# Scattering token numbers instead of token rows for a mixture of experts, and placing the skew rows in nine groups

## The chip, the cores and the metric

The kernel runs on one core of one Trainium2 chip. The metric is the device time of one execution in microseconds (us), the median of several runs; one further execution was taken with the hardware profiler, and every number of the trace comes from that one.

## The reference

Three transformer layers and a last rotation work on x of shape (4, 512, 288), so 2048 tokens of 288 numbers in float32. Each layer has attention with 16 heads and a feed-forward part of width 1152, both modulated by a condition. Only layer 0 matters to the change, where the feed-forward part is a mixture of 4 experts, and each token goes to its best 2:

```python
xn = _modulate(_ln(x), sh_mlp, sc_mlp)
xf = xn.reshape(-1, C)
gate_logits = xf @ w_gate
topk_logits, topk_idx = jax.lax.top_k(gate_logits, TOP_K)      # TOP_K = 2
gates = jax.nn.softmax(topk_logits, axis=-1)
cw = jnp.sum(one_hot(topk_idx, NUM_EXPERTS) * gates[..., None], axis=1)
hmid = gelu(jnp.einsum('tc,ech->eth', xf, w1) + b1[:, None, :])
eo = jnp.einsum('eth,ehc->etc', hmid, w2) + b2[:, None, :]
moe = jnp.einsum('te,etc->tc', cw, eo).reshape(B, N, C)
return x + g_mlp[:, None, :] * moe
```

The last rotation needs two more things that are prepared during the layers. U is the orthogonal factor of a QR factorization of P (288 x 64), which GpSimd makes with 64 Householder reflectors. R is expm(A), where A (one 64 x 64 skew-symmetric matrix for each batch) has its 2016 entries above the diagonal from a small product with L3_cond_W.

## The kernel before

Five engines run their own programs, written out in order by hand, and meet at semaphores; nothing reorders them. SP (SyncE) issues nearly all DMAs, GpSimd (POOL in the profile) issues the indirect ones.

**Layer 0, attention.** Work goes in 16 groups (4 batches, 4 groups of heads). SP loads each group's stacks of q and k (load_stacks, L732 and L733) and puts the row maxima into them (place_max, L772); TensorE makes scores for the maximum (L1448) and for the softmax (L1462); ScalarE takes the exponential (L1223); TensorE multiplies with v (L1473). Layers 1 and 2 run the same code. In layer 0 alone ScalarE also issues clear_rows (L1210) once in each group: 16 DMAs that write zeros from UO, still empty then, over all 9728 rows of the buffer XSD ("moe_rows_d").

**Layer 0, routing.** For each batch in turn the normalized rows XMR are made, VectorE counts the slot of each token with each of its two experts (slots, L2185, which gives IDX), and GpSimd scatters the 1152-byte rows into XSD with 8 indirect DMAs of 128 rows (scatter, L944). The rows of an expert then lie together, and spare slots hold zeros. tile_table makes the first row and the expert of 11 tiles of 512 slots.

**Layer 0, experts.** The 11 tiles (TILES) have 9 units each (HM), 99 units j in all. SP loads a tile's rows with one DMA (load_rows, L622) into one of two buffers XROW, and its weights in thirds, each as soon as VectorE has split the third before (load_tile_w1, load_tile_w2). Iteration t of SP's loop loads for tile t + 2. VectorE's program, unit by unit: the low part of the hidden numbers (L2262); in unit 1 tile_tails of the next tile (L2245, the first reader of its rows) and tile_take of the tile before (L2271); in units 2 to 4 the rows' split (L2253); in units 2, 5 and 8 the low parts of the next tile's w1 thirds (L2375, L2376). It also makes the skew entries from unit 4 (SKEW_UNIT, L2424; the first waits for l3_W and what is loaded behind it), the expm steps from unit 64 (EXPM_UNIT; step 0 on TensorE is L1727), and adds the experts' outputs back: combine(k, b) (L2280) for the first two batches at units 49, 57, 82 and 88 (COMBINE_UNIT). SP stores each tile's output (store_tile, L645), and GpSimd gathers the outputs by token for the combines (gather, L954). READY says how many tiles must be stored for it.

GpSimd fills the rest of its time with the reflectors, each of some 20 small instructions that depend on one another and one DMA (L867). PIVOTS cuts the 64 reflectors into pieces between its other work: 0 to 11 before the scatters, 12 to 18 before gather(0,0), 19 before gather(1,0), 20 to 26 before gather(0,1), and so on.

The skew entries are stored to DRAM in iteration 4 and come back with 63 DMAs, one per row of the triangle, to UO (place_skew, L651): 21 at the end of each of SP's iterations 4, 5 and 6.

Of the kernel before, what the change touches and what calls it, by code (L numbers as in the profile page):

```python
# [54 lines left out]
SKEW_UNIT, EXPM_UNIT = 4, 64  # L55
FRONT_SKEW = 4
FRONT = 12 + 2 * FRONT_SKEW
PIVOTS = (0, 12, 19, 20, 27, 28, 64)
# [14 lines left out]
def build(nc, x, cond, layers, l3_P, l3_W, l3_b, out):  # L73
    ctx = ExitStack()
    with ctx:
# [72 lines left out]

        STRICT = at("strictly_behind", [P, P], F32, rb + 58368)
# [76 lines left out]
        IDX = new("row_slots", [P, NT, 2], U32)  # L226
        TBL = new("tile_table", [P, 24], I32)
# [28 lines left out]
        XSD = nc.dram_tensor("moe_rows_d", [MOE_ROWS, C], F32, kind="Internal").ap()  # L256
# [83 lines left out]
        s_sd = sem("rows_scattered")  # L340
        s_zr = sem("rows_cleared")
# [197 lines left out]
        def _(sp):  # L539
# [103 lines left out]
            def store_tile(t):  # L643
                sp.wait_ge(m_ev, TT * (t + 1))
                sp.dma_start(YD[N * t:N * t + N, :].rearrange("(t p) c -> p t c", p=P), T1[:, :, :]).then_inc(m_y, 16)  # L645
# [6 lines left out]

            def moe_loads():

                sp.wait_ge(s_tb, 1)
                e = tile_expert(1)
                sp.wait_ge(s_sd, 32 * 16)
                load_rows(0)
                load_tile_w1(1, 0, e)
                load_rows(1)  # L660
                load_tile_b2(1, e)
                for i in range(3):
                    if i >= 1:
                        load_tile_w1(1, i, e)
                    load_tile_w2(1, i, e)
# [5 lines left out]
                for t in range(TILES):  # L671
# [20 lines left out]
                    if t == 4:  # L692
                        sp.wait_ge(s_vc, 1)
                        sp.dma_start(VD.rearrange("b (p t) -> p b t", t=VT_), VC[:, :, :]).then_inc(s_vd, 16)
                        sp.wait_ge(s_vd, 16)
                        sp.wait_ge(s_zr, 16 * B * HG)
                    if 4 <= t <= 6:
                        place_skew(range(21 * (t - 4), 21 * (t - 3)))
# [137 lines left out]
        def _(gp):  # L836
# [80 lines left out]
            def route_constants():  # L917
# [4 lines left out]
                gp.wait_ge(s_cn, 2)  # L922
                gp.affine_select(out=STRICT[:, :], in_=STRICT[:, :], compare_op=ALU.is_gt, fill=0.0, base=0,
# [13 lines left out]
            def scatter(b):  # L937
                if b == 0:
                    gp.wait_ge(s_zr, 16 * B * HG)
                gp.wait_ge(s_xc, 3 * b + 3)  # L940
                gp.wait_ge(s_ix, b + 1)
                for t in range(TT):
                    for k in range(2):
                        gp.indirect_dma_start(out=XSD[:, :], out_offset=bass.IndirectOffsetOnAxis(ap=IDX[:, TT * b + t, k:k + 1], axis=0),  # L944
                                              in_=XMR[b][:, t, :], in_offset=None).then_inc(s_sd, 16)
# [37 lines left out]
            reflectors(PIVOTS[5], PIVOTS[6])  # L983
# [1688 lines left out]
```

## Time and profile before

| | us |
|---|---|
| median of 3 runs | 1828.39 |
| lowest, highest | 1827.14, 1837.69 |
| the profiled execution's own time | 1825.07 |
| its span | 1823.3 |
| PE busy in the span | 1567.6 (86%) |
| DVE busy | 1304.7 (72%) |
| ACT busy | 936.6 (51%) |
| POOL busy | 732.0 (40%) |

PE is TensorE, PEld its weight loads, DVE VectorE, ACT ScalarE. An engine's name with a q (SPq, ACTq) is its queue, where DMAs are issued. The busy time tells how full an engine is over the whole span; the stages have different limits, so the rows below look at stretches. Times in a timeline count from the start of the span.

### The profile page before, as it was taken

The numbers are of one execution on the slowest core, as the hardware profiler recorded it, in microseconds if no ns is written. First come the engines' busy times: TensorE is split into PE (matmuls) and PEld (weight loads), VectorE is DVE, ScalarE is ACT, GpSimd is POOL, SyncE is SP. The second block draws the span as 40 slices with busy tenths as digits, with TensorE's granted clock in tenths as the row PEclk, the third lists the DMA queues.
The fourth block names the chain that finished last, engine by engine and source line by source line (L and its number), as shares of the span: only waits on it lengthen the run. The fifth ranks groups of instructions, "written<-read, shape, count | busy, mean of one in ns | idle before, by whom it ended". The sixth has DMA issues, their size and how long they took to land.

```text
span 1823.3 us, 29022 instructions
## 1 busy us (share of the span) xinstructions
PE 1567.6 (86%) x9053; PEld 1005.1 (55%) x9053; DVE 1304.7 (72%) x2364; ACT 936.6 (51%) x1657; POOL 732.0 (40%) x1607
## 2 busy tenths in 40 slices
PE   6878787766499996999967999989899899988998
PEld 4622222355488885788743222368787322248885
DVE  7776566544679767566687888777897888867763
ACT  4636566524355654344643777742255577772222
POOL 0566510024566346750366666566676600000000
PEclk9989889987699999999978999999999899999999
DMA  6566645601665544442435333421105422400001
GB/s 171 129 168 109 109 103 105 116 27 53 167 178 129 163 145 100 98 111 81 138 83 152 75 78 78 94 41 5 18 4 167 109 79 78 127 1 1 1 1 52
DMA packets 133684, 166.06 MB, mean 91 GB/s; under 512 B 34354, under 2 KB 115236, under 8 KB 133433
## 3 DMA queue, kind: packets, MB, share of 16 engines
q1 hardware_dynamic: 111802, 139.71, 26.6%
q0 software_dynamic: 5120, 13.65, 7.1%
q10 hardware_dynamic: 16640, 11.21, 3.5%
q8 instruction: 61, 1.00, 0.2%
q14 instruction: 61, 0.50, 0.1%
HBM read 113.97 MB, written 46.13 MB: 88 GB/s over the span
## 4 chain that ended last, share of the span: by engine, by line
PE 52%; DVE 20%; DMA 8%; SPq 8%; issue 7%; ACT 3%; POOL 1%; another core or an unknown queue 0%; DVEq 0%; ACTq 0%; POOLq 0%
PE psum L1324 15%; PE psum L1473 7%; PE psum L1462 7%; PE psum L1448 6%; PE psum L1625 6%; PE psum L1711 4%; DMA k_stack<-qk_parts_d 3%; DVE minus_max L2029 2%; SPq L732 2%; SPq L733 2%; SPq L772 2%; DMA q_stack<-minus_max_t 1%; DVE bn L1937 1%; PE psum L1518 1%; DVE x_norm L1959 1%
## 5 line engine op out<-in xcount | busy, mean ns | idle before, releaser
L2029 DVE TENSOR_REDUCE minus_max<-psum 128x2 bf16<-128x1024 f32 x384 | 453.5, 1219 | 137.8 <-PE psum L1448 130.9
L1223 ACT ACTIVATE probs<-psum 128x512 f32<-128x512 f32 x768 | 419.7, 601 | 211.8 <-PE psum L1462 209.6
L1462 PE MATMUL psum<-q_stack,k_stack 109*128 109x512 bf16 x768 | 266.9, 395 | 15.6 <-DMA q_stack<-minus_max_t 8.6
L1448 PE MATMUL psum<-k_stack,q_stack 108*128 108x512 bf16 x720 | 228.2, 400 | 49.6 <-DMA k_stack<-qk_parts_d 39.8
L1324 PE MATMUL psum<-x_split,w_hi 128*128 128x512 f32 x684 | 254.5, 413 | 10.8 <-DVE x_tail L1976 3.7
L874 POOL TENSOR_TENSOR qr_m<-qr_m 64x8 f32<-64x8 f32 (+35 forms) x544 | 204.5, 376 | 42.6
L1462 PEld LDWEIGHTS psum<-q_stack,k_stack 109*128 109x128 bf16 x768 | 73.9, 99 | 260.9 <-ACT probs L1223 179.5
L1473 PE MATMUL psum<-probs,v_stage 128*32 128x512 f32 x1536 | 208.3, 616 | 1.1 <-ACT o_t L1204 1.1
L1324 PEld LDWEIGHTS psum<-x_split,w_hi 128*128 128x128 f32 x684 | 130.7, 191 | 39.0 <-issue 9.5
L869 POOL TENSOR_TENSOR qr_m<-qr_rows 64x288 f32<-64x288 f32 (+31 forms) x64 | 45.8, 716 | 248.5 <-DMA qr_rows<-qr_rows 248.5
L1448 PEld LDWEIGHTS psum<-k_stack,q_stack 108*128 108x128 bf16 x720 | 69.0, 100 | 131.7 <-issue 40.2
L1324 PE MATMUL psum<-x_split,w_lo 128*128 128x512 f32 x342 | 136.3, 398 | 0.0
L1134 ACT ACTIVATE hid_f<-psum 128x512 f32<-128x512 f32 x99 | 59.2, 598 | 141.4 <-PE psum L1324 128.5
L1279 ACT ACTIVATE hid_f<-psum 128x512 f32<-128x512 f32 x72 | 42.9, 596 | 168.9 <-PE psum L1324 164.0
L1625 PE MATMUL psum<-w_hi,hid_hi 128*128 128x288 f32 x396 | 118.7, 300 | 11.8 <-DVE branch L2271 8.4
L2262 DVE TENSOR_TENSOR hid_lo<-hid_f,hid_hi 128x512 fp32r<-128x512 f32 x99 | 74.7, 755 | 66.6 <-ACT hid_hi L1099 61.4
L1625 PE MATMUL psum<-w_hi,hid_lo 128*128 128x288 f32 x396 | 117.7, 297 | 0.0
L1625 PE MATMUL psum<-w_lo,hid_hi 128*128 128x288 f32 x396 | 117.7, 297 | 0.0
L1324 PE MATMUL psum<-x_split,wqkv_hi 128*128 128x512 f32 (+1 forms) x240 | 94.7, 436 | 25.5 <-DVE qk_r L2014 22.1
L1711 PE MATMUL psum<-w_hi,hid_hi 128*128 128x288 f32 x288 | 87.1, 303 | 3.8 <-DVE hid_lo L2391 3.3
L1625 PEld LDWEIGHTS psum<-w_hi,hid_hi 128*128 128x128 f32 x396 | 75.3, 190 | 19.8 <-issue 10.9
L1711 PE MATMUL psum<-w_lo,hid_hi 128*128 128x288 f32 x288 | 85.2, 296 | 0.0
(354 smaller groups left out, 3242.1 us busy)
## 6 DMA issues: line engine op xcount, KB each, us to landing
qk_parts_d<-qk_parts SPq DMA_DIRECT2D x36, 384.0 KB
raw_b<-in_L_cond_w SPq DMA_DIRECT2D x30, 432.0 KB, 3.4
raw_a<-in_L_cond_w SPq DMA_DIRECT2D x30, 384.0 KB
moe_rows_d<-skew_upper ACTq DMA_DIRECT2D x16, 684.0 KB, 9.9
q_stack<-qk_parts_d SPq DMA_DIRECT2D x48, 216.0 KB
k_stack<-qk_parts_d SPq DMA_DIRECT2D x48, 216.0 KB
q_stack<-qk_parts_d SPq DMA_DIRECT2D x48, 144.0 KB
k_stack<-qk_parts_d SPq DMA_DIRECT2D x48, 144.0 KB
```

Source lines behind the costliest of these rows:

```text
L869: step(gp.tensor_tensor(QM1[:, 0, 0:n], rows, pivot, ALU.mult))
L874: step(gp.tensor_tensor(QM1[:, :, 0:h], QM1[:, :, 0:h], QM1[:, :, n - h:n], ALU.add))
L1134: act.activation(HF[:, j % 2, :], bk(j % 2), ACT.Gelu_apprx_tanh).then_inc(m_g, 1)
L1223: act.activation(PE_[:, v // 4, v % 4, :], psum[:, score_bank(v), :], ACT.Exp, scale=SCALE).then_inc(s_e, 1)
L1324: i = pe.matmul(dst, a, r, start=(n == 0), stop=(n == len(terms) - 1))
L1448: mm = pe.matmul(psum[:, 2 * (u % 2) + j, :], Q6[0:STK, g, u // 2, P * qt:P * qt + P], K6[0:STK, g, u // 2, :], start=True, stop=True)
L1462: pe.matmul(psum[:, score_bank(v), :], K6[0:STK + 1, g % 4, h, P * kt:P * kt + P], Q6[0:STK + 1, g % 4, h, :], start=True, stop=True).then ...
L1473: mm = pe.matmul(psum[32 * h:32 * h + 32, 6, :], VST[:, g % 4, kt, h, :], PE_[:, kt, h, :], start=(kt == 0), stop=(kt == TT - 1))
L1625: mm = pe.matmul(psum[:, 4 + q, 0:C], h[:, m % 3, c], w[:, m, :], start=(m == 0 and n == 0), stop=(m == HM - 1 and n == 2))
L1711: mm = pe.matmul(psum[:, 4 + t, 0:C], h[:, m % 3, c], w[:, m, :], start=(m == 0 and n == 0), stop=(m == HM - 1 and n == 2))
L2029: dve.tensor_reduce(MX[:, g % 2, 2 * u:2 * u + 2], psum[:, o:o + 2, :], AX.X, ALU.max, negate=True).then_inc(s_mx, 1)
L2262: dve.tensor_tensor(HL[:, m % 3, :], HF[:, j % 2, :], HH[:, m % 3, :].bitcast(F32), ALU.subtract).then_inc(m_h, 1)
```

## The change

- XSD is gone. The normalized rows are stored in token order with four plain DMAs (XTD), and the scatter writes 4-byte token numbers (TID, from an iota) into a small table SLD of 9728 slots. One DMA of SP clears SLD at the start; clear_rows is gone.
- SP loads a tile's 512 token numbers (load_tokens in place of load_rows), four to a partition, and GpSimd gathers the rows from XTD with four indirect DMAs per tile (gather_rows). Slots lie otherwise in the tile, and store_tile stores accordingly.
- GpSimd's order in the expert stage: gather_rows(t) for each tile, with one or two reflectors after each (PIVOTS new), gather(0,0) after the rows of tile 7 and gather(1,0) after those of tile 8.
- place_skew comes in nine groups of seven rows, between weight loads of iterations 4 to 6; its wait for the clear is gone. EXPM_UNIT goes from 64 to 66.

```diff
-SKEW_UNIT, EXPM_UNIT = 4, 64
+SKEW_UNIT, EXPM_UNIT = 4, 66
-PIVOTS = (0, 12, 19, 20, 27, 28, 64)
+PIVOTS = (0, 12, 13, 15, 17, 19, 20, 21, 22, 23, 24, 25, 64)
...
-            def load_rows(t):
+            def load_tokens(t):
                 if t >= 2:
-                    sp.wait_ge(m_tr, 3 * (t - 1))
-                sp.dma_start(XROW[t % 2][:, :, 0:C], XSD[tile_rows(t), :].rearrange("(t p) c -> p t c", p=P)).then_inc(m_x[t % 2], 16)
+                    sp.wait_ge(m_x[t % 2], 16 * TT * (t // 2))
+                sp.dma_start(TIX[t % 2][:, :], SLD[tile_rows(t), :].rearrange("(p t) o -> p (t o)", t=TT).bitcast(U32)).then_inc(m_ix[t % 2], 16)
...
+            def skew_rows(t, i):
+                if (t, i) == (4, 0):
+                    sp.wait_ge(s_vc, 1)
+                    sp.dma_start(VD.rearrange("b (p t) -> p b t", t=VT_), VC[:, :, :]).then_inc(s_vd, 16)
+                    sp.wait_ge(s_vd, 16)
+                if 4 <= t <= 6:
+                    first = 21 * (t - 4) + 7 * i
+                    place_skew(range(first, first + 7))
+
             def moe_loads():
+                for b in range(B):
+                    sp.wait_ge(s_xc, 3 * b + 3)
+                    sp.dma_start(XTD[N * b:N * b + N, :].rearrange("(t p) c -> p t c", p=P), XMR[b][:, :, :]).then_inc(s_xd, 16)
                 sp.wait_ge(s_tb, 1)
                 e = tile_expert(1)
                 sp.wait_ge(s_sd, 32 * 16)
-                load_rows(0)
-                load_tile_w1(1, 0, e)
-                load_rows(1)
+                load_tokens(0)
+                load_tokens(1)
...
                         load_tile_w1(t + 2, 0, e)
-                        load_rows(t + 2)
+                        load_tokens(t + 2)
                         load_tile_w2(t + 2, 0, e)
+                        skew_rows(t, 0)
                         load_tile_w1(t + 2, 1, e)
+                        skew_rows(t, 1)
                         load_tile_w2(t + 2, 1, e)
+                        skew_rows(t, 2)
                         load_tile_w1(t + 2, 2, e)
...
+            sp.wait_ge(s_cst, 2)
+            sp.dma_start(SLD.rearrange("(p n) o -> p (n o)", p=D3), UO[:, :, :].rearrange("p b d -> p (b d)")[:, 0:MOE_ROWS // D3].bitcast(I32)).then_inc(s_zr, 16)
...
+            def gather_rows(t):
+                if t == 0:
+                    gp.wait_ge(s_xd, 16 * B)
+                if t >= 2:
+                    gp.wait_ge(m_tr, 3 * (t - 1))
+                gp.wait_ge(m_ix[t % 2], 16 * (t // 2 + 1))
+                for q in range(TT):
+                    gp.indirect_dma_start(out=XROW[t % 2][:, q, 0:C], out_offset=None, in_=XTD[:, :],
+                                          in_offset=bass.IndirectOffsetOnAxis(ap=TIX[t % 2][:, q:q + 1], axis=0)).then_inc(m_x[t % 2], 16)
...
-            reflectors(PIVOTS[1], PIVOTS[2])
-            gp.wait_ge(s_iy, 1)
-            gather(0, 0)
-            reflectors(PIVOTS[2], PIVOTS[3])
-            gather(1, 0)
-            reflectors(PIVOTS[3], PIVOTS[4])
+            gather_rows(0)
+            gather_rows(1)
+            for t in range(2, TILES):
+                gather_rows(t)
+                if t == 7:
+                    gp.wait_ge(s_iy, 1)
+                    gather(0, 0)
+                if t == 8:
+                    gather(1, 0)
+                reflectors(PIVOTS[t - 1], PIVOTS[t])
             gather(0, 1)
-            reflectors(PIVOTS[4], PIVOTS[5])
+            reflectors(PIVOTS[TILES - 1], PIVOTS[TILES])
             gather(1, 1)
...
-            def clear_rows(bb, g):
...
-                    if v == 4 and l == 0:
-                        clear_rows(B - 1 if first else bb, HG - 1 if first else g - 1)
```

## Rows read from the trace of the kernel before

**Rows 1.** Busy time by stretch: attention 0, attention 1; clock, DMA share, GB/s.

```profile
116.30:365.90 249.60, 201.42 (x1031) 61.10 (x1029) 153.71 (x179) 146.53 (x271) 73.11 (x196) 0.88 0.60 111
993.50:1185.20 191.70, 186.25 (x1031) 59.04 (x1031) 156.56 (x182) 145.00 (x271) 115.24 (x312) 0.98 0.36 79
```

**Rows 2.** Groups by line, same stretches: busy, mean ns, idle before.

```profile
L1448 PE MATMUL psum<-k_stack,q_stack 108*128 108x512 bf16 x224 | 74.6, 417 | 38.2 <-DMA k_stack<-qk_parts_d 38.1
...
L1448 PE MATMUL psum<-k_stack,q_stack 108*128 108x512 bf16 x224 | 68.6, 388 | 1.0 <-DMA k_stack<-qk_parts_d 0.6 <-DVE minus_max L2029 0.4
```

**Rows 3.** DMA issues in attention 0: count, size, median us to landing.

```profile
moe_rows_d<-skew_upper ACTq DMA_DIRECT2D x9, 684.0 KB, 9.7
...
q_stack<-minus_max_t SPq DMA_DIRECT2D x33, 1.0 KB, 3.0
```

**Rows 4.** DMA issues in attention 1, the same columns.

```profile
q_stack<-minus_max_t SPq DMA_DIRECT2D x49, 1.0 KB, 1.7
```

**Rows 5.** Timeline at the end of the scatters: start, duration in us.

```profile
472.97 1.63 POOL L944 DMA_INDIRECT moe_rows_d<-moe_x,row_slots  x1 [0.30 <-issue]
...
476.08 0.39 SPq L622 DMA_DIRECT2D tile_rows<-moe_rows_d  x1
...
480.39 0.84 DVE L2245 COPY tile_rows<-tile_rows 128x128 f32<-128x128 f32 x2 [1.58 <-DMA tile_rows<-moe_rows_d]
```

**Rows 6.** Timeline, VectorE and TensorE at the wait for l3_W.

```profile
507.72 0.46 DVE L2424 SCALAR_TENSOR_TENSOR l_junk<-l_w,silu_c_all 126x288 f32<-126x288 f32 x1 [4.91 <-DMA skew_bias<-in_L_cond_b]
...
509.47 0.40 PE L1625 MATMUL psum<-w_hi,hid_hi 128*128 128x288 f32 x1 [1.30 <-DVE hid_lo L2262]
```

**Rows 7.** L954 by line (duration ns min/median/max), and one in the timeline.

```profile
L954 POOL DMA_INDIRECT moe_y<-moe_out_d,row_places x16: 942/1136/1812, 628.0 to 829.1; - x16
...
671.28 0.96 POOL L954 DMA_INDIRECT moe_y<-moe_out_d,row_places  x1 [0.30 <-issue]
```

**Rows 8.** Timeline, starts of reflectors: number 13 and 18, and two neighbours.

```profile
489.11 0.68 POOL L867 DMA_DIRECT2D qr_rows<-qr_rows  x1 [0.29 <-POOL qr_rows L897]
...
586.08 0.63 POOL L867 DMA_DIRECT2D qr_rows<-qr_rows  x1 [0.29 <-POOL qr_rows L897]
...
725.38 0.63 POOL L867 DMA_DIRECT2D qr_rows<-qr_rows  x1 [0.29 <-POOL qr_rows L897]
...
739.64 0.62 POOL L867 DMA_DIRECT2D qr_rows<-qr_rows  x1 [0.29 <-POOL qr_rows L897]
```

**Rows 9.** Timeline of SP's queue: tile 3's first weights, tile 3's rows.

```profile
531.77 0.37 SPq L629 DMA_DIRECT2D raw_a<-in_L_cond_w  x1
...
535.38 0.40 SPq L622 DMA_DIRECT2D tile_rows<-moe_rows_d  x1
```

**Rows 10.** Timeline of VectorE: combine(0,0); the split before combine(1,0), and it.

```profile
665.17 1.80 DVE L2280 SCALAR_TENSOR_TENSOR moe_y<-moe_y,logits,gate_mlp 128x288 f32<-128x288 f32 x4
...
690.27 0.56 DVE L2376 TENSOR_TENSOR w_tail<-raw_a,w_tail 33x384 fp32r<-33x384 f32 x1
...
692.89 1.80 DVE L2280 SCALAR_TENSOR_TENSOR moe_y<-moe_y,logits,gate_mlp 128x288 f32<-128x288 f32 x4
```

**Rows 11.** Chain that ended last: seven products after the skew wait, and next.

```profile
732.34 3.28 PE psum L1324 x7
...
738.64 1.84 PE psum L1324 x7
```

**Rows 12.** Timeline: the last skew rows on SP's queue, TensorE's first reader.

```profile
717.19 13.33 SPq L651 DMA_DIRECT2D skew_upper<-skew_d  x21
...
731.71 0.63 PE L1727 MATMUL psum<-ident,skew_upper 64*64 64x64 f32 x4 [15.47 <-DMA skew_upper<-skew_d]
```

**Rows 13.** Timeline: VectorE's tile_tails of tiles 8, 9 and 10.

```profile
717.61 0.45 DVE L2245 COPY tile_rows<-tile_rows 128x128 f32<-128x128 f32 x2
...
775.34 0.35 DVE L2245 COPY tile_rows<-tile_rows 128x128 f32<-128x128 f32 x2
...
817.01 0.36 DVE L2245 COPY tile_rows<-tile_rows 128x128 f32<-128x128 f32 x2
```

More of the change, by code:

```diff
@@ L147, in build @@
         HL = at("hid_lo", [P, 3, N], F32R, rb + 49920)
+        TIX = [at(f"tile_tokens{i}", [P, TT], U32, xo + 32256 + 32 * i) for i in range(2)]
         STRICT = at("strictly_behind", [P, P], F32, rb + 58368)
@@ L226, in build @@
         IDX = new("row_slots", [P, NT, 2], U32)
+        TID = at("token_numbers", [P, NT], I32, rb + 51200)
         TBL = new("tile_table", [P, 24], I32)
@@ L255, in build @@
         SCD = nc.dram_tensor("silu_d", [B, C], F32, kind="Internal").ap()
-        XSD = nc.dram_tensor("moe_rows_d", [MOE_ROWS, C], F32, kind="Internal").ap()
+        XTD = nc.dram_tensor("moe_rows_d", [TOK, C], F32, kind="Internal").ap()
+        SLD = nc.dram_tensor("slot_tokens_d", [MOE_ROWS, 1], I32, kind="Internal").ap()
         YD = nc.dram_tensor("moe_out_d", [TILES * N, C], F32, kind="Internal").ap()
@@ L339, in build @@
         s_iy = sem("places_made")
-        s_sd = sem("rows_scattered")
-        s_zr = sem("rows_cleared")
+        s_sd = sem("tokens_scattered")
+        s_xd = sem("moe_rows_stored")
+        s_zr = sem("slots_cleared")
+        m_ix = [sem(f"tile_tokens_loaded{i}") for i in range(2)]
         m_x = [sem(f"tile_rows_loaded{i}") for i in range(2)]
@@ L644, in store_tile @@
                 sp.wait_ge(m_ev, TT * (t + 1))
[L645 removed]
+                sp.dma_start(YD[N * t:N * t + N, :].rearrange("(p t) c -> p t c", t=TT), T1[:, :, :]).then_inc(m_y, 16)
             def place_skew(rows):
@@ L691, in moe_loads @@
                         load_k288(RAWP, layers[1]["out_w"], layers[1]["out_b"], s_rb)
[L692 to L698, printed above, removed]
                 store_tile(TILES - 1)
@@ L922, in route_constants @@
                 gp.wait_ge(s_cn, 2)
+                gp.iota(TID[:, :], pattern=[[P, NT]], base=0, channel_multiplier=1).then_inc(s_cn, 1)
                 gp.affine_select(out=STRICT[:, :], in_=STRICT[:, :], compare_op=ALU.is_gt, fill=0.0, base=0,
@@ L938, in scatter @@
                 if b == 0:
-                    gp.wait_ge(s_zr, 16 * B * HG)
-                gp.wait_ge(s_xc, 3 * b + 3)
+                    gp.wait_ge(s_zr, 16)
+                    gp.wait_ge(s_cn, 4)
                 gp.wait_ge(s_ix, b + 1)
@@ L943, in scatter @@
                     for k in range(2):
-                        gp.indirect_dma_start(out=XSD[:, :], out_offset=bass.IndirectOffsetOnAxis(ap=IDX[:, TT * b + t, k:k + 1], axis=0),
-                                              in_=XMR[b][:, t, :], in_offset=None).then_inc(s_sd, 16)
+                        gp.indirect_dma_start(out=SLD[:, :], out_offset=bass.IndirectOffsetOnAxis(ap=IDX[:, TT * b + t, k:k + 1], axis=0),
+                                              in_=TID[:, TT * b + t:TT * b + t + 1], in_offset=None).then_inc(s_sd, 16)
+            def gather_rows(t):
[7 more added lines that the diff above has]
+                                          in_offset=bass.IndirectOffsetOnAxis(ap=TIX[t % 2][:, q:q + 1], axis=0)).then_inc(m_x[t % 2], 16)
             def gather(k, b):
@@ L982, in _ @@
                     gather(k, b)
-            reflectors(PIVOTS[5], PIVOTS[6])
+            reflectors(PIVOTS[TILES], PIVOTS[TILES + 1])
             scale_rows()
@@ L1204, in o_t @@
                 act.activation(OT[:, bass.ds(i, 1), :].rearrange("p o n -> p (o n)"), bk(6), ACT.Copy).then_inc(s_ot, 1)
-            def clear_rows(bb, g):
-                rows = XSD.rearrange("(o r) c -> o (r c)", o=B)[bass.ds(bb, 1), :].rearrange("o (p a n) -> (o p) a n", p=D3, a=D3)
-                n = MOE_ROWS * C // (B * D3 * D3)
-                zeros = UO[:, :, :].rearrange("p b d -> p (b d)")[:, 0:n].unsqueeze(1).to_broadcast([D3, D3 // 4, n])
-                act.dma_start(rows[:, D3 // 4 * g:D3 // 4 * (g + 1), :], zeros).then_inc(s_zr, 16)
             def attention(l, bb, g, first=False):
                 i = 4 * bb + g
-                if l == 0 and first:
-                    act.wait_ge(s_cst, 2)
                 for v in range(16):
@@ L1576, in ranks @@
                 if b == 0:
-                    pe.wait_ge(s_cn, 3)
+                    pe.wait_ge(s_cn, 4)
                 mine = RK[:, TT * b:TT * b + TT, :]
@@ L2242, in tile_tails @@
             def tile_tails(t):
-                dve.wait_ge(m_x[t % 2], 16 * (t // 2 + 1))
+                dve.wait_ge(m_x[t % 2], 16 * TT * (t // 2 + 1))
                 for r in range(2):
```

3 lines of the change are left out of this document (1 added, 2 removed).

## The prediction

> **What bounds the kernel now.** I read the page's slices first: TensorE is at work nearly throughout, so only holes in its work are worth anything, stage by stage. Then the view by stretches, laid over the three attentions, which do the same work: layer 0's takes 249.6 us, layer 1's 191.7 us, at 111 against 79 GB/s and a granted clock of 0.88 against 0.98 [rows 1]. The view by line says why: in layer 0 the products of L1448 stand 38.1 us waiting for k_stack, in layer 1 0.6 us [rows 2]. What only layer 0 has is clear_rows: one 684 KB store per group, 9.7 us to land, and beside it the 1 KB max rows take 3.0 us to land in place of 1.7 [rows 3, 4]. Last the expert stage, read as a timeline: here TensorE and VectorE run close together, VectorE executes its waits in order, and three places matter: the start of the first tile, a wait for l3_W, a wait for the skew rows.
>
> **The change part by part.** All terms are made against the profiled execution, 1825.07 us (span 1823.3); the median of the runs shown is 1828.39.
>
> *The clear goes.* Sixteen stores of 684 KB become one of 39 KB (9728 numbers of 4 bytes), issued by SP at the start, far from its reader. Attention 0 should take what attention 1 takes: 249.6 - 191.7 = -57.9 us. The other end is the direct wait alone, -38.1 [rows 2]. Layer 1 has GpSimd's reflectors and the same loads beside it, and nothing else in layer 0 differs, so I take the first end, -57.9.
>
> *Tokens scattered, rows stored.* The 32 indirect DMAs stay 32 and each is built for 128 rows, so GpSimd's time for them stays; only bytes shrink. The four plain stores of moe_x are queued on SP, which has nothing to issue until the last scatter has landed [rows 5]; behind them stands s_tb, later still. One iota is added where GpSimd waits anyway. 0 us. If 4-byte writes land later than the 1.5 us seen (474.60 to 476.08), everything below starts later; bound 0 to +1.5.
>
> *The first tile.* Before: one load, issued 476.08, seen by VectorE at 480.39 [rows 5]. After: a token load (1.7 us to land, as other 1 KB DMAs [rows 4]) and 0.3 for the waits, four indirect DMAs with 0.30 between (at 0.96, VectorE being idle: 5.0 us), about 2 to land (1.5 seen for the last scatter): 485.1 or later, +5. VectorE waits at unit 4 for l3_W until 507.72 whatever the tile does, 4.91 us, of which TensorE feels 1.30 [rows 6]; that, and the backlog after it, hides part. I take +3 from here on. From the same rows comes the slack used below: TensorE runs on 4.91 - 1.30 = 3.6 us after VectorE stops.
>
> *Rows gathered by GpSimd in the loop.* This is the new wait. VectorE's tile_tails(t) waits for GpSimd's gather_rows(t), in GpSimd's queue behind reflectors, and the combines wait behind both. A set of four indirect DMAs costs 4 x (1.14 + 0.30) = 5.8 us [rows 7]. A reflector takes (586.08 - 489.11) / 5 = 19.4 us while VectorE is busy, 14.3 us while it stands (725.38 to 739.64) [rows 8]. A tile takes about 31.7 us; after gather_rows(3), (4) and (5) stand two reflectors each: 2 x 18 + 5.8 = 42 us. GpSimd falls behind. The chain: SP issues tile 3's rows 3.6 us after its first weight load, at 535.38 [rows 9]; plus 3 for the start, 1.7 landing and 0.3: 540.4. From there to combine(0,0) GpSimd has six sets (rows of 3 to 7, outputs of the first batch), 34.8 us, and seven reflectors (13 to 19), at 18 each (between the ends, nearer the busy one, as VectorE stands about a third of the time) 126 us, and 2 to land: 703.2. The combine now starts at 665.17 [rows 10]: VectorE is 38.0 us late. TensorE keeps 3.6 of that and loses about 2 when it restarts at the lower clock (the seven products after the skew wait took 3.28 us, 1.84 six microseconds later [rows 11]): +36.4, the +3 included. With reflectors at 14.3 it is 12.1 us late instead (+10.5), at 19.4 it is 47.8 (+46).
>
> *The second combine*, combine(1,0), stands one unit after VectorE splits the first w1 third of tile 7. SP loads tile 8's w1 third after that split, then tile 8's tokens; GpSimd gathers tile 8's rows, and only then the outputs for this combine. Chain from the split's end: 3.6 + 1.7 + 0.3 + 5.8 + 5.8 + 2 = 19.2 us. Now it starts 692.89 - 690.83 = 2.06 us after it [rows 10]. 17.1 late, minus 3.6, plus 2: +15.5. This one needs no backlog; the order alone makes it. Later combines come out on time (gather(0,1) within 1 us), and three reflectors more stay for the end, where GpSimd is idle in the page's last eight slices. 0 us.
>
> *Skew rows in nine groups, expm two units later.* SP issues the last 21 rows in one piece of 13.33 us, ending 730.5, and TensorE stands 15.47 us for them [rows 12]. After, seven rows (4.2 us) stand between weight loads, the last before tile 8's third w1 load; each weight third has about a tile, 31 us, as cover, and with unit 66 the rows have landed. VectorE's interval between tile_tails(8) and (9) is 57.7 us, the next, also with nine expm steps, 41.7 [rows 13]: -16.1. What is late next there is VectorE, within a microsecond or two. SP's wait for s_vd moves within tile 4 only.
>
> Sum: 1825.07 - 57.9 + 36.4 + 15.5 - 16.1 = 1803.0. The runs stand 2 to 3 us above the profiled execution: 1805.
>
> **A rule against the change.** Indirect DMAs took 1.14 us in the median and up to 1.81 beside VectorE's work [rows 7]. The Trainium skill (SBUF — State Buffer, "SBUF: two separate sides") says that GpSimd cannot write descriptors while VectorE runs an operation that takes their shared port pair, and in its section on the bandwidth-pool intuition gives about 3.1 us in place of 0.62 for such a DMA. An estimate by that page, 4 x 3.4 = 13.6 us a set, adds 7.8 us to each of eight sets, 1867 us; this trace shows nothing so long.
>
> **The rivals.**
> A. *GpSimd keeps up.* Reflectors run at 14.3 us since VectorE stands more: +10.5 in place of +36.4, 1779. For it: a feedback of that sign exists. Against: 14.3 was seen with VectorE wholly idle.
> B. *Descriptors starve.* Each indirect DMA at the 1.81 us of the row: a set takes 8.4, +2.6 on six sets and +5.2 on combine(1,0)'s two: 1805 + 21 = 1826, no change.
> C. *Slower: the clear is not what stretches attention 0.* Place: load_stacks of layer 0; price 57.9; the kernel is slower from the point where less than 36 us of the 57.9 come back (36.4 + 15.5 - 16.1), and with none 1863. Against it: the wait that grows is for a DMA, and the landing of the small max rows grows with it [rows 2 to 4]. That the change doesn't do what it says would look the same.
>
> **How the numbers follow.** A difference within 1% (18.3 us; faster means under 1810.1) can't be told from none. Forecast 0.70, own range 1786 to 1826, about two thirds of it under 1810 (0.46 faster, 0.24 same). A 0.13, faster. B 0.10, same. C 0.07, slower. Faster 0.59, same 0.34, slower 0.07. The range takes in A and B and most of the bounds: 1778 to 1834.
>
> **What would show it.** Attention 0 at 190 to 195 us with no wait of L1448 for k_stack. VectorE's tile_rows copies on time for tiles 1 to 3, 1 to 3 us late for 4, some 12 late for 5 and 6, their releaser the indirect DMA. A wait before combine(0,0) of some 15 us and before combine(1,0) of about 17. No TensorE wait for skew_upper. It is wrong if reflectors take another time than 18 us, if landing among weight loads takes much over 2 us, or if attention 0 stays above 200.

## The result, and the profile after

The kernel after the change takes 1820.76 us (median of 7 runs, 1814.76 to 1825.75) beside 1833.43 for the kernel before (7 runs): a ratio of 0.9935, 95% interval 0.9909 to 0.9961. It is faster by 12 to 13 us, 0.65%; the forecast was 1805. That is less than the 1% which the prediction took as the least that counts as faster (under 1810.1), but the interval lies wholly under 1. The profiled execution took 1822.24 us, its span 1820.5.

The page of the kernel after, packets and memory traffic (13.5 MB less written than before):

```profile
DMA packets 112388, 152.57 MB, mean 84 GB/s; under 512 B 36802, under 2 KB 92148, under 8 KB 112137
...
HBM read 114.00 MB, written 32.62 MB: 81 GB/s over the span
```

The kernel after by stretch, attention 0 and attention 1, columns as in [rows 1]:

```profile
115.00:305.50 190.50, 184.97 (x1027) 58.45 (x1029) 154.81 (x181) 144.71 (x271) 73.96 (x198) 0.99 0.36 87
980.10:1171.20 191.10, 185.03 (x1031) 58.34 (x1031) 155.40 (x183) 144.97 (x271) 116.92 (x315) 0.99 0.37 79
```

Its maximum products in attention 0 by line, and the max rows among the DMA issues there, against [rows 2, 3]:

```profile
L1466 PE MATMUL psum<-k_stack,q_stack 108*128 108x512 bf16 x224 | 68.2, 386 | 2.1 <-DMA k_stack<-qk_parts_d 2.0
```

```profile
q_stack<-minus_max_t SPq DMA_DIRECT2D x60, 1.0 KB, 1.7
```

Attention 0 is now as long as attention 1: from the first exponential to the end of the last both take 191.1 us (the first row above stops half a microsecond short of it), where the old attention 0 took 249.6. The wait for k_stack went from 38.1 to 2.0 us, the granted clock from 0.88 to 0.99, the landing of the max rows from 3.3 (over the whole of attention 0; 3.0 in the part of it that [rows 3] shows) to 1.7 us. At the start of the last exponential of attention 0, which is called its end from here on (305.4 us; 365.3 before), the kernel is 59.9 us ahead. What follows gives most of it back. The timeline of the kernel after, from the last scatter to VectorE's first tile_tails, against [rows 5]:

```profile
411.81 1.48 POOL L958 DMA_INDIRECT slot_tokens_d<-token_numbers,row_slots  x1 [0.30 <-issue]
...
420.73 1.50 SPq L627 DMA_DIRECT2D tile_tokens<-slot_tokens_d  x2
...
423.11 1.01 POOL L968 DMA_INDIRECT tile_rows<-moe_rows_d,tile_tokens  x1 [9.82 <-DMA tile_tokens<-slot_tokens_d]
...
433.51 0.36 DVE L2263 COPY tile_rows<-tile_rows 128x128 f32<-128x128 f32 x2 [14.08 <-issue]
```

SP, which waits for all scatters to land, goes on 420.73 - 413.29 = 7.4 us after the last one ends. Before, with 1152-byte rows, it was 476.08 - 474.60 = 1.5 us. From the end of attention 0 to tile_tails(0) it takes 128.1 us in place of 115.1: +13.0. The scatters account for 4.5 of it (they land 5.9 us later and are issued 1.4 us sooner). The other 8.5 lie between SP's first load and VectorE. Part of them is a slow landing: GpSimd's last gather for tile 0, and the DMA engines while these rows land (columns as in [rows 1]):

```profile
426.93 0.95 POOL L968 DMA_INDIRECT tile_rows<-moe_rows_d,tile_tokens  x1 [0.30 <-issue]
```

```profile
424.00:433.50 9.50, 0.00 (x0) 0.00 (x0) 0.00 (x0) 0.00 (x0) 6.75 (x8) 0.50 1.02 301
```

The last gather ends at 427.88 and VectorE starts at 433.51, 5.6 us later; where VectorE waits for rows later (tiles 4 to 6) it is 1.8 to 2.7 us. SP's weight loads for tile 1 and GpSimd's rows for tile 1 are issued in the same microseconds, and the 16 DMA engines are full (share 1.02). Before the change the rows were the first load that SP issued there.

Then VectorE in the expert stage, kernel after. The view of waits, 425 to 760 us (total, times, longest); then the timeline of its late tile_tails (tiles 4, 5, 6) and of combine(0,0) and combine(1,0):

```profile
DVE moe_y L2298 <- DMA moe_y<-moe_out_d,row_places: 28.0, 2, 16.3
DVE tile_rows L2263 <- DMA tile_rows<-moe_rows_d,tile_tokens: 17.5, 3, 7.6
```

```profile
540.94 0.36 DVE L2263 COPY tile_rows<-tile_rows 128x128 f32<-128x128 f32 x2 [2.72 <-DMA tile_rows<-moe_rows_d,tile_tokens]
...
581.41 0.36 DVE L2263 COPY tile_rows<-tile_rows 128x128 f32<-128x128 f32 x2 [7.63 <-DMA tile_rows<-moe_rows_d,tile_tokens]
...
621.46 0.36 DVE L2263 COPY tile_rows<-tile_rows 128x128 f32<-128x128 f32 x2 [7.18 <-DMA tile_rows<-moe_rows_d,tile_tokens]
...
649.18 1.80 DVE L2298 SCALAR_TENSOR_TENSOR moe_y<-moe_y,logits,gate_mlp 128x288 f32<-128x288 f32 x4 [11.66 <-DMA moe_y<-moe_out_d,row_places]
...
693.64 1.80 DVE L2298 SCALAR_TENSOR_TENSOR moe_y<-moe_y,logits,gate_mlp 128x288 f32<-128x288 f32 x4 [16.35 <-DMA moe_y<-moe_out_d,row_places]
```

The tiles stand 40.5 and 40.0 us apart where 31.7 is their own length: that is GpSimd's pace, two reflectors and a set of gathers. Both combines wait for their DMA. From tile_tails(0) to (8) it takes 717.01 - 433.51 = 283.5 us, before 717.61 - 480.39 = 237.2: +46.3. The first three of these tiles are 2.9 us shorter than before, though, because VectorE's wait of 4.91 us for l3_W [rows 6] is gone. The same instruction, kernel after:

```profile
457.72 0.45 DVE L2442 SCALAR_TENSOR_TENSOR l_junk<-l_w,silu_c_all 126x288 f32<-126x288 f32 x1
```

So the tiles behind them cost 49.2 us.

TensorE's first reader of the skew rows, and tile_tails of tiles 8, 9 and 10, kernel after, against [rows 12, 13]:

```profile
725.15 0.41 PE L1745 MATMUL psum<-ident,skew_upper 64*64 64x64 f32 x4
```

```profile
717.01 0.35 DVE L2263 COPY tile_rows<-tile_rows 128x128 f32<-128x128 f32 x2
...
756.43 0.35 DVE L2263 COPY tile_rows<-tile_rows 128x128 f32<-128x128 f32 x2
...
798.10 0.36 DVE L2263 COPY tile_rows<-tile_rows 128x128 f32<-128x128 f32 x2
```

The 15.47 us wait is gone and tile 8's interval is 39.4 in place of 57.7 us: -18.3. But behind tile 10 the change adds. The stretch from tile_tails(10) to attention 1, kernel before, then kernel after (columns as in [rows 1]):

```profile
817.00:993.50 176.50, 143.41 (x869) 114.38 (x867) 129.87 (x239) 80.64 (x141) 72.59 (x137) 0.90 0.42 115
```

```profile
798.10:980.10 182.00, 145.06 (x901) 115.11 (x899) 132.60 (x242) 80.44 (x142) 85.91 (x156) 0.92 0.42 115
```

It is 5.5 us longer and holds 901 - 869 = 32 more products of TensorE. An expm step has 16: these are the two steps that EXPM_UNIT = 66 moves behind tile 10. They left tile 8's interval, whose -18.3 so counts for -12.8.

Up to the start of attention 1 this makes -59.9 + 13.0 + 46.3 - 18.3 + 5.5 = -13.4 us. The rest of the two profiled executions differs by +10.6, nearly all between attention 1 and 2 (250.4 us before, 260.4 after), where the change touches nothing. The runs' medians say -12.7, as the sum up to attention 1 does; a second execution of the kernel before settles it (below).

### The profile page after: what moved, and what is told of

The parts are those of the page before. It is cut to its first block, busy times and chain, and to the rows that moved or that the text cites. A ratio compares the mean times of both kernels' runs of the same rounds, so it can differ in the third digit from the quotient of the medians.

```text
span 1820.5 us, 29035 instructions
## 1 busy us (share of the span) xinstructions
PE 1563.5 (86%) x9053; PEld 1013.2 (56%) x9053; DVE 1303.2 (72%) x2364; ACT 935.3 (51%) x1657; POOL 778.8 (43%) x1652
## 4 chain that ended last, share of the span: by engine, by line
PE 52%; DVE 18%; issue 10%; DMA 6%; POOL 6%; SPq 4%; ACT 3%; DVEq 0%; POOLq 0%; ACTq 0%
PE psum L1342 14%; PE psum L1491 8%; PE psum L1480 8%; PE psum L1466 7%; PE psum L1729 4%; PE psum L1643 3%; DVE minus_max L2047 2%; DMA k_stack<-qk_parts_d 2%; PE psum L1403 2%; DMA qr_rows<-qr_rows 1%; POOL qr_m L887 1%; POOL tile_rows L968 1%; DVE bn L1955 1%; SPq L745 1%; PE psum L1536 1%
## 5 line engine op out<-in xcount | busy, mean ns | idle before, releaser
L1342 PE MATMUL psum<-x_split,w_hi 128*128 128x512 f32 x684 | 258.3, 419 | 11.3 <-DVE x_tail L1994 4.4
L1480 PE MATMUL psum<-q_stack,k_stack 109*128 109x512 bf16 x768 | 260.3, 386 | 8.2 <-ACT probs L1243 5.3
L1466 PE MATMUL psum<-k_stack,q_stack 108*128 108x512 bf16 x720 | 220.8, 389 | 14.2 <-DVE minus_max L2047 9.0
L1491 PE MATMUL psum<-probs,v_stage 128*32 128x512 f32 x1536 | 203.9, 604 | 1.1 <-ACT o_t L1232 1.1
L1643 PE MATMUL psum<-w_hi,hid_hi 128*128 128x288 f32 x396 | 121.5, 307 | 50.4 <-DVE hid_lo L2280 25.6
L1162 ACT ACTIVATE hid_f<-psum 128x512 f32<-128x512 f32 x99 | 59.3, 599 | 151.6 <-PE psum L1342 122.5
L1643 PE MATMUL psum<-w_lo,hid_hi 128*128 128x288 f32 x396 | 119.9, 303 | 0.0
L1643 PEld LDWEIGHTS psum<-w_hi,hid_hi 128*128 128x128 f32 x396 | 77.3, 195 | 59.3 <-issue 28.0
L968 POOL DMA_INDIRECT tile_rows<-moe_rows_d,tile_tokens x44 | 49.0, 1113 | 110.2 <-DMA tile_tokens<-slot_tokens_d 81.7
L1729 PE MATMUL psum<-w_hi,hid_hi 128*128 128x288 f32 x288 | 88.1, 306 | 4.4 <-DVE hid_lo L2409 3.2
```

The lines of the kernel that those rows point to most:

```text
L968: gp.indirect_dma_start(out=XROW[t % 2][:, q, 0:C], out_offset=None, in_=XTD[:, :], in_offset=bass.IndirectOffsetOnAxis(ap=TIX[t % 2][:, q ...
L1162: act.activation(HF[:, j % 2, :], bk(j % 2), ACT.Gelu_apprx_tanh).then_inc(m_g, 1)
L1342: i = pe.matmul(dst, a, r, start=(n == 0), stop=(n == len(terms) - 1))
L1466: mm = pe.matmul(psum[:, 2 * (u % 2) + j, :], Q6[0:STK, g, u // 2, P * qt:P * qt + P], K6[0:STK, g, u // 2, :], start=True, stop=True)
L1480: pe.matmul(psum[:, score_bank(v), :], K6[0:STK + 1, g % 4, h, P * kt:P * kt + P], Q6[0:STK + 1, g % 4, h, :], start=True, stop=True).then ...
L1491: mm = pe.matmul(psum[32 * h:32 * h + 32, 6, :], VST[:, g % 4, kt, h, :], PE_[:, kt, h, :], start=(kt == 0), stop=(kt == TT - 1))
```

## The experiments

Each ratio is against the kernel before, run on the same chip. "The tile stretch" is tile_tails(0) to tile_tails(8).

**1. after_again: the changed kernel once more. 12. before_again: the kernel before once more, profiled.** No edit.

> The changed kernel, unchanged, for a second trace. In its first trace it stood 14.3 us ahead of the kernel before at the end of attention 1 and only 4.7 us ahead at the start of attention 2. If that loss belongs to the execution (VectorE bound stretch at a lower granted clock), the stretch from the last exponential of attention 1 to the first of attention 2 comes back to about 250 us, as before, from 260.4. If it belongs to the kernel (three more reflectors beside VectorE's work), it is 258 to 262 again. Ratio to before 0.991 to 0.996 either way.

> The kernel before, unchanged, for a second trace. In its first trace the stretch between attention 1 and attention 2 took 250.4 us, in those of nine variants 253.7 to 261.3, skew_only among them (259.9), which has before's reflectors. If that first execution was a short one there, this one takes 255 to 262 and its time is near 1830; if it is again 249 to 252, something of the skew part, in all nine variants, costs some 8 us later.

after_again: 0.9938 (0.9918 to 0.9958), 1818.13 us, the same waits within 2 us. before_again: 1831.12 us, span 1829.4. The stretch between attention 1 and 2 in the kernel before, first execution; in its second; and in the kernel after:

```profile
1184.50:1435.00 250.50, 219.57 (x1259) 182.38 (x1259) 204.02 (x428) 100.86 (x174) 168.79 (x365) 0.96 0.26 57
```

```profile
1181.80:1439.00 257.20, 219.71 (x1257) 182.93 (x1258) 207.15 (x427) 101.46 (x174) 170.78 (x382) 0.95 0.26 55
```

```profile
1170.60:1431.00 260.40, 223.06 (x1258) 185.77 (x1256) 208.89 (x425) 100.57 (x173) 178.17 (x390) 0.94 0.27 56
```

The same kernel gives 250.4 and 257.2 there. Over all the kernels run, whatever their edit, it lay between 253.3 and 261.3 but for that first execution. So most of the 10 us that the profiled pair shows there is scatter between executions, and the first profile of before was a short one. About 2 us (after_again has 259.1) may belong to the change; that stays open.

**2. no_reflectors: GpSimd does none of the reflectors 12 to 24 in the tile loop, but at its end.**

```diff
-PIVOTS = (0, 12, 13, 15, 17, 19, 20, 21, 22, 23, 24, 25, 64)
+PIVOTS = (0,) + (12,) * 11 + (64,)
```

> The changed kernel with all 52 later reflectors after the expert stage and none in its loop. My theory, GpSimd's chain of two reflectors per tile makes the rows late: VectorE's waits for tile_rows (17.5 us in three places) go to zero, combine(0,0) still waits some 10 us because of the order alone, combine(1,0) stays near 16; the stretch from the first to the ninth tile_tails falls from 283.5 to 258 to 268 us, ratio 0.980 to 0.987. Rival, the indirect DMAs' own descriptor writing beside VectorE is what delays: waits and stretch stay within 5 us, ratio 0.991 to 0.996. A loss is possible at the end if U comes late: the last of 52 reflectors would end near 1680, the first reader is at 1750.

0.9924 (0.9895 to 0.9954), 1815.9 us. VectorE's waits, and GpSimd at the rows of tile 7:

```profile
DVE moe_y L2298 <- DMA moe_y<-moe_out_d,row_places: 31.5, 2, 16.2
```

```profile
619.23 0.94 POOL L968 DMA_INDIRECT tile_rows<-moe_rows_d,tile_tokens  x1 [30.30 <-DMA tile_tokens<-slot_tokens_d]
...
624.23 0.94 POOL L978 DMA_INDIRECT moe_y<-moe_out_d,row_places  x1 [0.30 <-issue]
```

The 17.5 us of waits for tile_rows are gone and the tile stretch is 263.5 us, 20 less, as expected; the time, expected at 0.980 to 0.987, is not. Both combine waits stay, 15.4 and 16.2 us, though GpSimd is idle: it stands 30.3 us for the token numbers of tile 7, and gather(0,0) stands behind that. So the order alone holds back both combines, not the second only. The time hardly moved, because later stretches grew beside after_again: tile 9's interval from 41.7 to 47.7, and the end after attention 2 from 201.2 to 205.6 us, with the last reflector's DMA at 1657.6 in place of about 1470. In tile 9 TensorE waits 3.4 us for a step of VectorE's expm and then works at the lower clock; the stretch right after that wait:

```profile
764.60:771.00 6.40, 6.35 (x31) 5.56 (x32) 1.37 (x2) 1.61 (x3) 0.00 (x0) 0.55 0.10 30
```

Its 331 products of tile 9 take 44.3 us in place of 41.7, which with the wait is the whole 6.0. No reflector runs in this tile. VectorE and ScalarE both stand until 763.9 us there, and the trace names no engine or DMA of this core that they wait for; why stays open.

**3. outputs_earlier: the outputs are gathered one tile earlier in GpSimd's queue.**

```diff
-                if t == 7:
+                if t == 6:
                     gp.wait_ge(s_iy, 1)
                     gather(0, 0)
-                if t == 8:
+                if t == 7:
                     gather(1, 0)
```

> The changed kernel with gather(0,0) one tile earlier (after the rows of tile 6) and gather(1,0) after the rows of tile 7; reflectors as they are. My theory, the combines wait behind a later tile's tokens in the order alone: the two waits before the combines (11.7 and 16.3 us) fall to under 5 together, the waits for tile_rows stay or grow by a set's 5.8 us; stretch of the first nine tile_tails 283.5 to 263 to 272, ratio 0.984 to 0.989. Rival, GpSimd's total work in these tiles is the bound, whatever the order: the waits only move to tile_rows, stretch 278 or more, ratio 0.991 or more.

0.9823 (0.9785 to 0.9861), 1794.25 us. VectorE's waits, same stretch:

```profile
DVE tile_rows L2263 <- DMA tile_rows<-moe_rows_d,tile_tokens: 32.0, 4, 13.9
```

No combine waits any more. Of the 32.0 us, 13.9 are the first tile's wait, which the kernel after has too (14.1, put down to "issue" there); tiles 4 to 6 wait 18.1 us, as before this edit (17.5). So the waits did not move to the rows: the tile stretch is 259.4 us, 24 less than in the kernel after, and the rival (GpSimd's work as a whole is the bound) falls.

**4. both_queue: edits 2 and 3 together.**

> Both edits together: no reflectors in the expert loop, output gathers one tile earlier. By my two terms (36.4 and 15.5 us less the 3 of the start) the stretch of the first nine tile_tails comes back to the 237 of the kernel before, at most 243, and the ratio is 0.968 to 0.975. By the rival (descriptor writing itself) it stays above 255 and the ratio above 0.98.

0.973 (0.9708 to 0.9752), 1780.73 us. The tile stretch is 234.4 us, 2.8 less than before the change, which is what the first three tiles give: the two together account for all that was lost. The later costs are back: tile 9 takes 47.9 us, with the same wait of 3.4 us, and the end 206.6.

**5. tokens_early: all tiles' token numbers are loaded ahead of the loop, each tile into a piece of its own.**

```diff
+                for t in range(2, TILES):
+                    load_tokens(t)
                 for t in range(TILES):
...
-                        load_tokens(t + 2)
```

> The changed kernel with the token numbers of tiles 2 to 10 all loaded before the loop, into buffers of their own, so that no gather waits for SP's weight loads. In the changed kernel GpSimd waited 2.5 us for tile 7's tokens and 15.5 us for tile 8's. My theory: the wait before combine(1,0) falls from 16 us to under 5, the others stay (reflectors), ratio 0.984 to 0.988. Rival, the combine waits for GpSimd's backlog in any case: ratio 0.991 or more. SP spends some 10 us more before the loop; if weights come late by that, TensorE waits in tile 1.

0.9866 (0.9821 to 0.991), 1804.74 us. VectorE's waits:

```profile
DVE tile_rows L2262 <- DMA tile_rows<-moe_rows_d,tile_tokens: 25.4, 3, 14.5
...
DVE moe_y L2297 <- DMA moe_y<-moe_out_d,row_places: 10.6, 1, 10.6
```

combine(1,0) is on time with the outputs where the change puts them: its wait came from SP's position for the token load. combine(0,0) still waits 10.6, now for the backlog of reflectors: GpSimd goes from a reflector to tile 7's rows and from there to these outputs with 0.3 us between. The first tile's 14.5 us are in the row above; tiles 5 and 6 wait 11.0 in place of 14.8, tile 4 no longer. The tile stretch is 263.9 us, 20 less, but tile 8 takes 43.1 us in place of 39.4.

**6. wide_slots: a slot of the table takes 64 bytes in place of 4, only the first number of which is used.**

```diff
+WIDE = 16
-        SLD = nc.dram_tensor("slot_tokens_d", [MOE_ROWS, 1], I32, kind="Internal").ap()
+        SLD = nc.dram_tensor("slot_tokens_d", [MOE_ROWS, WIDE], I32, kind="Internal").ap()
...
-                                              in_=TID[:, TT * b + t:TT * b + t + 1], in_offset=None).then_inc(s_sd, 16)
+                                              in_=TID[:, TT * b + t:TT * b + t + WIDE], in_offset=None).then_inc(s_sd, 16)
```

> The changed kernel with 64 bytes for each slot in place of 4: each indirect DMA scatters 128 pieces of 64 bytes (the token number first, junk behind it), the clear and the token loads are 16 times as large. In the changed kernel SP sees the scatters landed 7.4 us after GpSimd's last one, against 1.5 us with 1152-byte rows. Theory, small writes are slow for their size: with 64 bytes the gap falls to 2 to 5 us. Rival, what counts is that they are 128 writes below some size, or that stores of the rows stand between: the gap stays at 6 to 9 us. In the time at most 5 us, since VectorE waits for l3_W at unit 4 anyway: ratio 0.990 to 0.996.

0.9896 (0.9869 to 0.9922), 1812.77 us. The timeline of wide_slots from the last scatter on:

```profile
411.60 1.48 POOL L959 DMA_INDIRECT slot_tokens_d<-token_numbers,row_slots  x1 [0.30 <-issue]
...
414.24 1.49 SPq L628 DMA_DIRECT2D tile_tokens<-slot_tokens_d  x2
...
426.84 0.36 DVE L2264 COPY tile_rows<-tile_rows 128x128 f32<-128x128 f32 x2 [7.62 <-DMA tile_rows<-moe_rows_d,tile_tokens]
```

The scatters are issued at the same pace and the last ends at 413.08. SP goes on 1.2 us later, not 7.4, with 16 times the bytes written. The edit changes two things at once, the size of a write and the distance to its neighbours (16 slots of 4 bytes lie within 64); which of the two makes the 4-byte case slow was not separated. The first tile starts 7.0 us earlier after attention 0 (121.1 us), and the tile stretch stays 283.5: all seven come through. That is +6.0 beside the kernel before, near the +5 of the forecast, but partly by luck: the rows again land late, 4.8 us after tile 0's last gather.

**7. with_clear: the kernel after, with the 16 stores of zeros put back at their old place in ScalarE's queue, to a buffer that nobody reads.** The work is the reference's and these stores beside it.

```diff
+                    if v == 4 and l == 0:
+                        clear_rows(B - 1 if first else bb, HG - 1 if first else g - 1)
```

> The changed kernel with the sixteen zero stores put back at their old places, now into a buffer that nothing reads. My theory, these stores alone stretch attention 0: from 190.5 back to 245 to 250 us, with L1466 waiting some 38 us for k_stack, ratio to before 1.020 to 1.028. Rival, attention 0 was stretched by something else that the change took away: it stays under 200 us, ratio 0.991 to 0.997.

1.0183 (1.014 to 1.0226), 1863.32 us. Attention 0 of with_clear by stretch, and its maximum products:

```profile
116.50:349.90 233.40, 200.37 (x1027) 62.32 (x1029) 154.75 (x181) 145.87 (x271) 73.07 (x197) 0.91 0.59 118
```

```profile
L1479 PE MATMUL psum<-k_stack,q_stack 108*128 108x512 bf16 x224 | 73.8, 413 | 25.7 <-DMA k_stack<-qk_parts_d 25.7
```

The stores alone bring back 42.9 of the 58.5 us of attention 0, most of the wait for k_stack and of the lower clock, and all of that, (1.0183 - 0.9935) x 1834 = 45 us, reaches the end. It is less than the 55 to 60 expected. The old attention 0 itself varies: 249.6 and 248.0 us in the two executions of the kernel before and 245.2 in skew_only, which changes nothing up to there. So 11 to 16 us of it are not explained by these stores in this buffer; why stays open.

**8. skew_only: the kernel before with the nine groups and EXPM_UNIT = 66 alone.**

```diff
-SKEW_UNIT, EXPM_UNIT = 4, 64
+SKEW_UNIT, EXPM_UNIT = 4, 66
...
+                        skew_rows(t, 0)
                         load_tile_w1(t + 2, 1, e)
+                        skew_rows(t, 1)
                         load_tile_w2(t + 2, 1, e)
+                        skew_rows(t, 2)
                         load_tile_w1(t + 2, 2, e)
```

> The kernel before with the skew part of the change alone: nine groups between weight loads, expm from unit 66. TensorE's wait of 15.5 us for skew_upper goes, the interval between tile_tails of tiles 8 and 9 falls from 57.7 to about 41, 16 us gained: ratio 0.990 to 0.993. Rival, another wait takes its place (VectorE behind, or weights late because SP is held): the interval stays above 50, ratio 0.996 or more.

0.996 (0.9936 to 0.9983), 1824.95 us: 7 us, between 3 and 12, and not the 16 expected. tile_tails of tiles 8, 9 and 10:

```profile
715.77 0.40 DVE L2251 COPY tile_rows<-tile_rows 128x128 f32<-128x128 f32 x2
...
756.75 0.77 DVE L2251 COPY tile_rows<-tile_rows 128x128 f32<-128x128 f32 x1
...
798.91 0.36 DVE L2251 COPY tile_rows<-tile_rows 128x128 f32<-128x128 f32 x2
```

Tile 8's interval falls from 57.7 (56.9 in before_again) to 41.0 us. The stretch behind tile 10 is 182.3 in place of 176.5 and 177.1 us, as in the kernel after. So those 5 us belong to this part of the change, and the net is near -10, not -16.

**9. one_each: outputs_earlier, and one reflector after each tile's rows.**

```diff
-PIVOTS = (0, 12, 13, 15, 17, 19, 20, 21, 22, 23, 24, 25, 64)
+PIVOTS = (0, 12, 13, 14, 15, 16, 17, 18, 19, 20, 21, 22, 64)
```

> The changed kernel with the output gathers one tile earlier and one reflector after each tile's rows (none of the pairs after tiles 3 to 5), 42 left for the end. A set and a reflector take about 24 us, a tile 31.6. My theory: no wait for tile_rows and none before the combines, stretch of the first nine tile_tails 234 to 238 us as with no reflectors at all, but without the 5 us that the two kernels with all reflectors at the end lost after attention 2 (their last reflector began at 1623 and 1658, beside VectorE's work there; here near 1510): ratio 0.966 to 0.971. Rival, any reflector between the gathers delays them: stretch 245 or more, ratio 0.975 or more.

0.9676 (0.965 to 0.9703), 1776.75 us. The tile stretch is 235.2 us, tile 9's interval 41.7 and the end 202.1: all of both_queue's gain in the tile stretch without its later costs.

**10. one_each_wide: one_each with the 64-byte slots.**

> The same with 64 bytes for each slot. The scatter's landing took 1.2 us instead of 7.4 with it, the first tile came 7 us earlier: ratio 0.962 to 0.968 if this adds up, 0.966 to 0.971 if VectorE's wait for l3_W takes it back.

0.9633 (0.96 to 0.9666), 1766.81 us, the fastest of all: 3.7% under the kernel before. Its interval overlaps that of one_each; in the profiled pair the first tile comes 4.3 us sooner after attention 0 and the tile stretch is 2.1 us longer. VectorE's only wait for rows or outputs in its tiles is the first:

```profile
DVE tile_rows L2264 <- issue: 7.8, 1, 7.8
```

**11. clear_first: skew_only, with the 16 stores of zeros issued by SP ahead of attention 0.**

```diff
+            for k in range(B * HG):
+                clear_rows(k)
             for l in range(LAYERS):
...
-                        clear_rows(B - 1 if first else bb, HG - 1 if first else g - 1)
```

> The kernel before with the skew part of the change, and its sixteen zero stores issued by SP back to back before attention (after the loads of the start) in place of one per group. The same 11.2 MB are written. If it is their place beside the stacks' loads that costs, attention 0 takes 190 us and what precedes it gets longer by less than the 54 to 58 us gained, by 10 to 30: ratio 0.965 to 0.985. If the bytes cost the same anywhere: ratio 0.99 or more.

1.0144 (1.0118 to 1.0171), 1860.28 us. SP's queue in clear_first, then attention 0 by stretch:

```profile
18.93 3.60 SPq L728 DMA_DIRECT2D silu_d<-silu_c  x3
22.58 101.00 SPq L734 DMA_DIRECT2D moe_rows_d<-skew_upper  x16
123.62 5.66 SPq L554 DMA_DIRECT2D raw_a<-in_L_cond_ada_w  x1
129.32 0.32 SPq L555 DMA_DIRECT2D raw_a<-in_L_cond_ada_b  x1
129.69 10.19 SPq L759 DMA_DIRECT2D qk_parts_d<-qk_parts  x3
```

```profile
214.00:403.00 189.00, 185.05 (x1028) 58.90 (x1031) 154.69 (x182) 144.48 (x270) 46.02 (x124) 0.99 0.34 86
```

Attention 0 itself takes 189 us: the same stores do nothing to it from elsewhere. But SP needs 101 us to issue them, 6.3 us each, and the q and k parts that attention waits for stand behind. The DMA engines in these 101 us:

```profile
22.60:123.60 101.00, 26.83 (x135) 20.12 (x133) 28.89 (x85) 19.34 (x34) 21.76 (x53) 0.66 1.13 98
```

They are full (share 1.13), and a store takes 31.6 us to land in the median. So it is not SP alone that is held up. Attention 0 starts at 214.4 in place of 116.3 us. Here the stores cost 98 us ahead of it, where 10 to 30 were expected, and give 56 to 60 back (skew_only's attention 0 takes 245.2 us, before's 249.6). Early stores from another queue, or in larger pieces (these move about 680 bytes a packet, 16640 packets for 11.21 MB in attention 0 of the kernel before), were not tried.

## Why the forecast was too low

The direction was right and the time is inside the range, but 1805 was 16 us too low: about 22 us of gain forecast, 12.7 measured. What went wrong is the path to the first tile: the scatters' landing was taken as unchanged and took 5.9 us more, and the gathered rows' landing was taken as 2 us and took 5.6. The work behind the first tile was sized well.

- *The clear goes, -57.9.* Right: -58.5 in attention 0. Rival C (the clear is not what stretches it) falls by with_clear and clear_first, though with_clear brings back 43 us only. The wait and clock that made it were named rightly; the last 11 to 16 us were not shown to be the clear's.
- *Tokens scattered, 0, bound 0 to +1.5.* This is the step that failed first. The landing was taken from 1152-byte rows [rows 5]; 4-byte writes into neighbouring slots need 7.4 us after the last scatter, 5.9 more, outside the bound that the forecast set. wide_slots shows that 64-byte slots take it away.
- *The first tile, +5, of which TensorE +3.* It came 13.0 us late: 4.5 by the scatters and 8.5, not 5, from SP's first load on. The forecast gave the rows 2 us to land, from the last scatter before the change; they took 5.6 with the DMA engines full of weight loads. The prediction had named this as a sign of being wrong ("if landing among weight loads takes much over 2 us"), and among the rows that VectorE waits for it came true here only. That the full engines are the reason is read from the trace, not tried. That VectorE waits for l3_W until 507.72 "whatever the tile does" was wrong too: SP issues that load behind its wait for the scatters, so it moves with them, and in the kernel after nothing waits for it. That gave 2.9 us back, where the forecast counted 2.
- *Rows gathered in the loop and the second combine, +36.4 and +15.5.* The size was right. Without the first tile's +3 the forecast had 33.4 + 15.5 = 48.9 us for these, and the trace has 49.2. From the end of attention 0 to tile_tails(8) it had 51.9 and the trace has 13.0 + 46.3 = 59.3; the difference, 7.4, is the first tile (13.0 - 2.9 = 10.1 in place of 3) but for 0.3. The places were named well, the waits less so: 2.7, 7.6 and 7.2 us at tiles 4 to 6 (forecast 1 to 3, then 12), 11.7 and 16.3 at the combines (15 and 17), 40 us a tile (42). But the cause of the first combine's part was only half seen. The forecast gave it to the reflectors; without them it still waits 15.4 us, since the token numbers of tile 7 come late. Both reasons stood at the same place: in the kernel after GpSimd waits 2.49 us for tile 7's tokens and 15.53 for tile 8's, as its timeline shows.

```profile
637.05 1.48 POOL L968 DMA_INDIRECT tile_rows<-moe_rows_d,tile_tokens  x1 [2.49 <-DMA tile_tokens<-slot_tokens_d]
...
681.85 1.15 POOL L968 DMA_INDIRECT tile_rows<-moe_rows_d,tile_tokens  x1 [15.53 <-DMA tile_tokens<-slot_tokens_d]
```

- *Skew rows, -16.1.* Mis-sized: tile 8 gave 18.3, but 5.5 came back behind tile 10. The two expm steps that move there were not costed. Their 32 products cost about 2.3 us (a step's sixteen 1.14 each); the other 3 us of that stretch were not settled.
- Rival A (GpSimd keeps up) did not happen. With the outputs one tile earlier it does at one reflector a tile, as one_each shows.
- Rival B (descriptors starve) did not happen. GpSimd's gathers of rows by line, kernel after (ns min/median/max):

```profile
L968 POOL DMA_INDIRECT tile_rows<-moe_rows_d,tile_tokens x44: 945/962/1779, 423.1 to 775.7; - x44
```

The median was 0.96 us, but half of them met an idle VectorE: those 22 took 0.95 us in the median, the 22 that lay beside a VectorE operation 1.17 and at most 1.78, as the 1.14 and 1.81 of [rows 7]. The 3.1 us of the Trainium skill (SBUF — State Buffer, the bandwidth-pool intuition) were seen in no run here: the longest indirect DMA of all traces took 1.96 us. Most of VectorE's operations beside them are TENSOR_TENSOR and SCALAR_TENSOR_TENSOR; whether the page's case ever arose in this kernel is not shown.

The sum of the misses: 7.4 us by the first tile and 3.3 by the skew part, less 2.0 by which the kernel was further ahead after attention 0, are the 8.7 between -22.1 and -13.4. Most of the rest of the distance in microseconds is that the kernel before had been read at 1828 and lay at 1833 over more runs.

## What to carry to other kernels

Taking bytes off a stage where loads are waited for gave all it promised; the loss was in a queue elsewhere. When a producer moves to another engine's queue, list what stands between its input and its consumer on both queues (here a token load behind weights, and outputs behind the next tile's rows), and move what is already ready ahead: moving the outputs one tile ahead was worth 1.1%, and three reflectors fewer in the loop another 1.5%. A load that is to be first must also be first on the DMA engines: here the first tile's rows came to share them with the next tile's weights. A step moved later is paid for where it lands, so cost it there too.

## What the runs showed of the hardware

- Small scattered writes into neighbouring slots land late. Four sets of eight indirect DMAs of 128 writes each, about 1.3 us apart within a set (1.4 to 1.8 at the end of the last set with 1152-byte rows), had all landed 7.4 us after the last for 4-byte writes, 1.2 us for 64-byte ones and 1.5 us for 1152-byte ones. The Trainium skill (DMA: Bandwidth & Descriptors, Specifications) says that under 512 bytes a transfer misses line rate and is a read-modify-write; the 4-byte case agrees in direction, the 64-byte case shows no such cost, so 512 is not the border here.
- A DMA of 684 KB that costs ScalarE's queue 0.63 us when it stands by itself holds SP's for 6.3 us when sixteen stand in a row, and everything queued behind them; the DMA engines are full then (share 1.13).
- Gathered rows landed 1.8 to 2.7 us after the last of four gathers at tiles 4 to 6, and 5.6 us after it at tile 0, where the DMA share was 1.02.
- The same 16 stores beside attention's loads stretch it by 43 us (with_clear) at a DMA share of 0.59; the kernel before, with 0.60, lost 54 to 58 us, not all of it shown to be theirs: a share far under 1 doesn't say that transfers cost nothing.
